# A graph layer with linear attention and expert layers on one core: where the expert jobs' results wait, and when they are scattered to the output

## The reference, cut to what matters

```
xn = layernorm(x)
x1 = x + gnn(xn, src, dst) + linear_attention(xn)
h  = layernorm(x1)
e  = argmax(h @ gate_w + gate_b)                   # one of 8 experts for each node
y  = (relu(h @ w1[e] + b1[e]) @ w2[e] + b2[e]) * prob[e]   # capacity 977 nodes an expert
out = x1 + nan_to_num(y)
```

## Time and profile before

| | |
|---|---|
| time, median of 3 runs | 1460.22 us (1460.05 to 1461.22) |
| profiled execution: its own time | 1454.21 us |
| span of its instructions | 1452.5 us |
| busy: TensorE, VectorE, ScalarE, GpSimd | 78%, 56%, 39%, 63% of the span |
| granted TensorE clock, mean | 0.914 |
| indirect DMAs: gathers, row scatters, result scatters | 784, 49, 54 |

### The profile page before, as it was taken

One profiled execution on the slowest core, in us unless ns is written; L12 is line 12 of the kernel. 1 busy time (PEld: TensorE's weight loads), 2 busy tenths in 40 slices (PEclk: granted clock), 3 DMA queues, 4 the chain that ended last, 5 costly groups with the idle time before them and its releaser, 6 DMA issues.

```text
span 1452.5 us, 34026 instructions
## 1 busy us (share of the span) xinstructions
PE 1138.5 (78%) x5961; PEld 809.4 (56%) x5962; DVE 818.0 (56%) x2766; ACT 560.9 (39%) x1458; POOL 918.9 (63%) x967
## 2 busy tenths in 40 slices
PE   2659977758778777888868888787888788888896
PEld 1437643534545445665545655565665666667885
DVE  5954432647657666666535555464665566656443
ACT  2843221322323234343423334343454444545342
POOL 3545776777777776767767676776766666751111
PEclk9569997879888989999989999899999999999998
DMA  8484333444545456545545455555555565555562
GB/s 250 139 230 154 103 106 99 146 125 146 150 143 152 146 154 190 170 140 182 163 135 162 153 178 174 166 178 164 180 171 167 183 197 165 172 161 164 162 181 83
DMA packets 143379, 231.83 MB, mean 160 GB/s; under 512 B 29824, under 2 KB 87329, under 8 KB 143248
## 3 DMA queue, kind: packets, MB, share of 16 engines
q0 software_dynamic: 42896, 115.65, 26.5%
q1 hardware_dynamic: 99118, 114.27, 25.6%
q10 hardware_dynamic: 1234, 0.66, 0.2%
HBM read 197.40 MB, written 35.08 MB: 160 GB/s over the span
## 4 chain that ended last, share of the span: by engine, by line
PE 29%; issue 26%; POOL 22%; DVE 8%; DMA 5%; ACT 4%; POOLq 3%; DVEq 2%; SPq 1%; ACTq 0%; PEldq 0%
POOL shared L587 21%; PE pY L1036 7%; PE pH L1045 6%; PE pA L915 6%; DMA shared<-table,idx 3%; DVE shared L1415 2%; PE pX L1013 1%; PE pT L967 1%; PE pQ L959 1%; DMA shared<-in_L_ffn_b_dram 1%; PE pD L973 1%; ACT w2s L651 1%; ACT w2s L646 1%; PE pH L895 1%; DVE shared L1421 1%
## 5 line engine op out<-in xcount | busy, mean ns | idle before, releaser
L587 POOL DMA_INDIRECT shared<-table,idx x784 | 766.8, 978 | 318.6 <-issue 272.4
L915 PE MATMUL pA<-shared,onehot 128*128 x976 | 281.6, 398 | 141.4 <-POOLq L567 79.9
L915 PEld LDWEIGHTS pA<-shared,onehot 128*128 x976 | 91.9, 98 | 320.0 <-issue 245.1
L1355 DVE TENSOR_TENSOR onehot<-tile_iota,dst_t 128x512 f32 x244 | 160.2, 694 | 105.8 <-PE pA L915 69.9
L1036 PE MATMUL pY<-w2s,shared 128*128 x864 | 208.3, 396 | 11.8 <-issue 9.0
L1045 PE MATMUL pH<-shared 128*128 128x128 f32 x1728 | 205.1, 278 | 6.6 <-DMA shared<-in_L_ffn_w_dram 6.6
L1045 PEld LDWEIGHTS pH<-shared 128*128 128x128 f32 x1728 | 204.0, 194 | 10.4 <-DMA shared<-in_L_ffn_w_dram 7.9
L1036 PEld LDWEIGHTS pY<-w2s,shared 128*128 128x128 f32 x864 | 165.7, 197 | 37.9 <-issue 15.7
L765 ACT ACTIVATE shared<-pH,b1s 128x128 f32<-128x128 f32 x432 | 122.2, 370 | 97.1 <-PE pH L1045 90.1
L700 ACT ACTIVATE shared<-pA 128x512 f32<-128x512 f32 x49 | 29.3, 597 | 272.2 <-PE pA L915 272.2
L1397 DVE TENSOR_SCALAR tile_iota<-tile_iota 128x128 f32<-128x128 f32 x48 | 12.7, 264 | 203.6 <-PE pA L915 203.6
(11 more groups left out here) (248 smaller groups left out, 1667.2 us busy)
## 6 DMA issues: line engine op xcount, KB each, us to landing
shared<-in_L_ffn_w_dram SPq DMA_DIRECT2D x108, 512.0 KB, 4.2
shared<-table,idx POOLq DMA_INDIRECT x784
w2s<-in_L_ffn_w_dram SPq DMA_DIRECT2D x8, 1024.0 KB, 6.8
rows<-rows_sb SPq DMA_DIRECT2D x7, 1040.0 KB, 14.6
shared<-rows SPq DMA_DIRECT2D x54, 130.0 KB
shared<-in_L_ffn_b_dram SPq DMA_DIRECT2D x54, 128.0 KB
shared<-in_x_dram SPq DMA_DIRECT2D x12, 512.0 KB, 8.7
table<-w2s SPq DMA_DIRECT2D x12, 512.0 KB, 3.1
```

The source lines that it names most:

```text
L587: g.indirect_dma_start(gathered[:, s * G + j, :], None, table[:, :], bass.IndirectOffsetOnAxis(ap=idx[:, q * G + j:q * G + j + 1], axis=0) ...
L915: m = pe.matmul(pA[:, :], onehot[:, n % OQ, j, :], gathered[:, (f % RQ) * G + j, :], start=False, stop=final and j == G - 1)
L1355: v.tensor_tensor(onehot[:, n % OQ, :, :], tile_iota[:, :].rearrange("p (a n) -> p a n", a=1).broadcast_to([P, G, P]), dst_t[:, bass.ds(ch ...
```

## The change

The results of the first 44 jobs (`KEPT = 44`: the 42 inside the steps and the tail's first two) are no longer written to the ring `fin`. VectorE writes the result of job j over `base` of tile j, which nobody reads any more by then, and its node numbers to column j of a wider `jtok`; these posts don't wait for a free buffer. GpSimd's `event` no longer ends with a `finish`. When the last row scatter has been issued, GpSimd scatters the 44 kept results one after another (`send_kept`), waiting only for each result and not for the scatter before. The ten jobs behind them use the ring of four as before; their `finish(r)` first waits until all earlier result scatters have landed.

```diff
+KEPT = J0 + LEAD - 2
...
-        jtok = sb("jtok", [P, FB], I32)
+        jtok = sb("jtok", [P, KEPT + FB], I32)
...
-            def finish(j):
-
-                g.wait_ge(S["fin_sc"], j * 16 + 16)
+            def finish(r):
+
+                g.wait_ge(S["fin_sc"], r * 16 + (KEPT + 1) * 16)
                 g.sem_inc(S["fin_free"], 1)
-                g.wait_ge(S["fin_ok"], j + 1)
+                g.wait_ge(S["fin_ok"], r + KEPT + 1)
                 hold(g, "pool_hold")
...
+            def send_kept(j):
+
+                g.wait_ge(S["fin_ok"], j + 1)
+                g.indirect_dma_start(out[:, :], bass.IndirectOffsetOnAxis(ap=jtok[:, j:j + 1], axis=0), base[:, j, :], None,
+                                     bounds_check=N - 1, oob_is_err=False).then_inc(S["fin_sc"], 16)
+
+            def event(t):
...
-                with g.If(T0 - 1 < t):
-                    finish(g.snap(done_r))
-                    g.reg_add(done_r, done_r, 1)
-                    g.sem_inc(S["pool_hold"], 1)
...
+            for j in range(KEPT):
+                send_kept(j)
             g.wait_ge(S["tail_ok"], 1)
-            end = g.value_load(last_job, min_val=J0, max_val=J0 + NX * JOBS)
-            with g.Fori(NT - T0, end + 1) as j:
-                finish(j)
+            end = g.value_load(last_job, min_val=J0 + LEAD - 1, max_val=J0 + NX * JOBS)
+            with g.Fori(0, end - (KEPT - 1)) as r:
+                finish(r)
...
-                def post(j):
+                def post(j, r=None):
...
-                    v.wait_ge(S["fin_free"], j + 1)
-                    v.sem_inc(S["dve_hold"], 1)
+                    if r is not None:
+                        v.wait_ge(S["fin_free"], j + 1)
+                        v.sem_inc(S["dve_hold"], 1)
...
-                    v.tensor_copy(jtok[:, bass.ds(j % FB, 1)], jrow[:, j % JB, C_TOK:C_TOK + 1].bitcast(I32))
-                    v.tensor_tensor(fin[:, j % FB, :], yc, jrow[:, j % JB, 0:D], ALU.add).then_inc(S["fin_ok"], 1)
+                    at_ = j if r is None else r % FB + KEPT
+                    done = base[:, j, :] if r is None else fin[:, r % FB, :]
+                    v.tensor_copy(jtok[:, bass.ds(at_, 1)], jrow[:, j % JB, C_TOK:C_TOK + 1].bitcast(I32))
+                    v.tensor_tensor(done, yc, jrow[:, j % JB, 0:D], ALU.add).then_inc(S["fin_ok"], 1)
...
-                v.sem_inc(S["fin_free"], FB - 1)
+                v.sem_inc(S["fin_free"], KEPT + FB - 1)
```

More of the change, by code:

```diff
@@ L517, in pick @@
                 g.sem_inc(S["pool_hold"], 1)
-            def finish(j):
-                g.wait_ge(S["fin_sc"], j * 16 + 16)
+            def finish(r):
+                g.wait_ge(S["fin_sc"], r * 16 + (KEPT + 1) * 16)
                 g.sem_inc(S["fin_free"], 1)
-                g.wait_ge(S["fin_ok"], j + 1)
+                g.wait_ge(S["fin_ok"], r + KEPT + 1)
                 hold(g, "pool_hold")
                 def send(b):
-                    g.indirect_dma_start(out[:, :], bass.IndirectOffsetOnAxis(ap=jtok[:, b:b + 1], axis=0),
+                    g.indirect_dma_start(out[:, :], bass.IndirectOffsetOnAxis(ap=jtok[:, KEPT + b:KEPT + b + 1], axis=0),
                                          fin[:, b, :], None,
                                          bounds_check=N - 1, oob_is_err=False).then_inc(S["fin_sc"], 16)
-                pick((g.snap(j % FB), 0), FB, send)
-            def event(t, done_r):
+                pick((g.snap(r % FB), 0), FB, send)
+            def send_kept(j):
[3 more added lines that the diff above has]
+            def event(t):
                 g.wait_ge(S["scat_done"], t * 16 + 16)
@@ L553, in load_end, with events @@
                 g.reg_add(reg, reg, -1)
-            def events(tile, tend, done_r, f):
+            def events(tile, tend, f):
                 with g.While(lambda: g.snap(tend) < f - LAG):
-                    event(g.snap(tile), done_r)
+                    event(g.snap(tile))
                     g.reg_add(tile, tile, 1)
@@ L572, in copy_idx, with gather @@
                 g.tensor_copy(idx[:, o:o + HALF], src_t[:, bass.ds((i % TURNS) * IDX + o, HALF)]).then_inc(S["idx_ok"], 1)
-            def gather(i, q, tile=None, tend=None, done_r=None):
+            def gather(i, q, tile=None, tend=None):
                 s = q % RQ
@@ L579, in gather @@
                 if q % 2 == 0 and not (first and q < RQ):
-                    events(tile, tend, done_r, f)
+                    events(tile, tend, f)
                 if q % RQ == 0:
@@ L601, in _ @@
             turns = g.value_load(rounds, min_val=TURNS, max_val=TURNS * NT)
-            with g.register("tile_no") as tile, g.register("tile_end") as tend, g.register("jobs_done") as done_r:
+            with g.register("tile_no") as tile, g.register("tile_end") as tend:
                 g.reg_mov(tile, 0)
-                g.reg_mov(done_r, 0)
                 load_end(tend, BEHIND)
                 for q in range(FIRST, BODY):
-                    gather(0, q, tile, tend, done_r)
+                    gather(0, q, tile, tend)
                 with g.Fori(1, turns) as i:
                     for q in range(BODY):
-                        gather(i, q, tile, tend, done_r)
+                        gather(i, q, tile, tend)
                 report(RQ - 1, turns * TRIPS * 16 * G)
                 with g.Fori(g.snap(tile), NT) as t:
-                    event(t, done_r)
+                    event(t)
+            for j in range(KEPT):
+                send_kept(j)
             g.wait_ge(S["tail_ok"], 1)
-            end = g.value_load(last_job, min_val=J0, max_val=J0 + NX * JOBS)
-            with g.Fori(NT - T0, end + 1) as j:
-                finish(j)
+            end = g.value_load(last_job, min_val=J0 + LEAD - 1, max_val=J0 + NX * JOBS)
+            with g.Fori(0, end - (KEPT - 1)) as r:
+                finish(r)
         @block.scalar
@@ L1650, in _ @@
                 plan(PLANNED + 1, 1.0)
-                with v.Fori(0, n) as i:
+                for i in range(LEAD - 1):
                     post(i + (J0 - 1))
                     plan(i + (PLANNED + 2), 1.0)
-                end = v.value_load(last_job, min_val=J0, max_val=J0 + NX * JOBS)
-                post(end)
+                with v.Fori(0, n - (LEAD - 1)) as r:
+                    post(r + KEPT, r)
+                    plan(r + (PLANNED + LEAD + 1), 1.0)
+                end = v.value_load(last_job, min_val=J0 + LEAD - 1, max_val=J0 + NX * JOBS)
+                post(end, v.snap(end - KEPT))
 _INS = ["x", "src", "dst", "L0_gnn_W", "L0_gnn_b", "L0_mix_wq", "L0_mix_bq", "L0_mix_wk", "L0_mix_bk", "L0_mix_wv", "L0_mix_bv",
```

## The result

The changed kernel takes 1446.7 us (median of 6 runs, 1443.8 to 1451.0), the kernel before beside it 1459.9 us (6 runs, 1451.4 to 1461.2). The ratio is 0.9917, with a 95% interval of 0.9891 to 0.9943: 13 us faster, where the prediction said 31. The time lies above the predicted range.

The account below looks back on a forecast made before the run. GpSimd, sending DMAs one after another, was taken to hold up TensorE until 1146 us, TensorE's own work after. Loop gain 34 less tail cost 3 gave 31 us off the 1460.2 us median: 1429.2 us, range 1417 to 1443.

Parts of the forecast that it names:

- the prediction's sum for the loop: Gain in GpSimd's loop from 650 to 1296 us: 19.9 to 924, 14.1 to 1146, 0 after, together 34 us.
- 19.9 were predicted up to 924 us: Loop, 650 to 924 us: 13 result scatters go, and all 19.9 us reach TensorE, which waits 34.9 us there.
- 14.1 predicted: Loop, 924 to 1146 us: TensorE gets back 7.5 us of relay waits and 6.6 us of weight waits.
- the 1.53 us each: GpSimd's busy and idle time per result scatter leaving the loop, 35 of them, 53.5 us; flag, counter and branch included.
- The tail: After the last row scatter: 44 kept scatters in a row cost 2.0 + 1.2 = 3 us, bounds 0 and 8.
- two mechanisms: In the tail: job 47 waits for the ring, TensorE 2.0 us late; scatter traffic slows four bias loads, 1.2 us.
- 2.0 predicted: In the tail: job 47's mask operation on VectorE is 6.0 us late, which makes TensorE 2.0 us late.
- 0.3 each: In the tail: scatter traffic adds 0.3 us to each of four bias loads, judged from the loop's weight loads.
- GpSimd never bound behind 1146 us: Rival on the loop: GpSimd bounds everywhere, all 35 scatters count, 53.5 - 3 = 50 us gained, 1410 us, 12%.
- The kept scatters went back to back: Rival on the tail: each kept scatter must land before the next, 2.8 us each, 24 us slower, 1484 us, 4%.
- The second rival: Loop, 924 to 1146 us: stalls recur in other steps, so 19.9 - 3 = 17 us gained, 1443 us, 13%.
- the four: All the rivals; the last: gathers are late for their landings, not GpSimd's time, 0 to 3 us slower, 1461, 3%.

Follow-up runs that it names:

- the kernel with 74 increments: The changed kernel with 74 idle semaphore increments, one instruction each, ahead of GpSimd's first gather: 1426.8 us, ratio 0.9829 to the kernel before.
- with 10 and with 60 increments: The kernel before with 10 or 60 idle semaphore increments ahead of GpSimd's first gather: 1455.5 us (ratio 0.9999) and 1471.8 us (ratio 1.0120).

## Why the prediction was wrong

**The size of the loop's gain was right for a kernel that was not the one built.** In the kernel with 74 increments TensorE's 38th step begins 35.1 us earlier than before; the prediction's sum for the loop was 34. By stage: its 24th step (892.72 us before) 20.1 us earlier, where 19.9 were predicted up to 924 us, and 14.9 more to the 38th (14.1 predicted), then nothing more: its 49th step is 34.8 us early. The events themselves freed less than the 1.53 us each, and as much in the kernel that was built: from the end of the gather ahead of an event to the start of the one behind it, 155.2 us for the last 35 events of the loop before, 118.8 after and 118.7 with 74 increments, 1.04 each; for the first 13 of them, which TensorE waits for, 54.5, 36.7 and 36.4 us, 1.39 each with 74. Cheaper turns than before (31.8 against 36.1 us) made up for part of it, so that the 35.1 us come so near to 34 is in part luck.

**The step that failed** is the sentence "The flag, the counter and one branch that leave GpSimd's loop are in the 1.53 us". It treats code that leaves a loop as time that leaves it, and the rest of the loop as unchanged. But with the branch gone from the seven event sites, the loop's head and its first gather came to lie elsewhere, and the turns up to frame 112 had a second stall. Turn by turn (excess after over before) that is 10.9 us up to frame 84, and TensorE's 12th step began 11.6 us late:
```profile
641.40 0.38 PE L938 MATMUL pA<-c 128*128 128x512 f16 x1
```
and before
```profile
629.75 0.38 PE L935 MATMUL pA<-c 128*128 128x512 f16 x1
```
From frame 98 to 140 the excess is 7.4 us, and the stage's 19.9 became 11.7 (the 24th step began as late as before, from 11.6 us behind); frames 154 and 168 add 4.4 us, and 14.1 became 10.1. Together 34 - 10.9 - 7.4 - 4.4 = 11.3 us were left, and the profile shows 10.1. Of the last 4.4 us at most 1.8 depend on the place: the two turns take 12.5 us after, 10.8 with 74 increments and 8.1 before. Why they are longer than before in that kernel too is open.

The stall ahead of the loop's head is in both kernels: after, the first instruction behind the branch back at frame 98 runs 4.1 us later, 1.56 us behind the start of a packet; before, 3.0 us later and 1.54 us behind one. The second stall made the difference.

**The tail** was mis-sized, 3 for 7 us (4 us against the 103.2 us that the kernel before takes with 10 and with 60 increments). Its two mechanisms are there. Job 47's mask operation waits for the ring, with 74 increments (for the earlier trace rows):
```profile
1370.62 0.29 DVE L1556 TENSOR_SCALAR finite<-shared 128x256 int32<-128x256 f32 x1 [6.07 <-POOLq L523]
```
and TensorE is 3.0 us later behind it (2.0 predicted; 0.5 in the profile after, where the jobs were late already). The bias loads were 0.8, 1.2 and 0.9 us slower in the profile after than before, 2.9 together, where 0.3 each had been taken from the loop's rows; before, the first two took (the third is in the earlier trace rows):
```profile
1360.11 3.93 DMA shared<-in_L_ffn_b_dram
...
1375.60 3.72 DMA shared<-in_L_ffn_b_dram
```
The loop's weight loads were a poor model for a bias load that the job hangs on. The third part was not foreseen: in 1330 to 1350 us TensorE's granted clock is 0.83 on the mean, 0.5 for 3.4 us from 1330.1 and for 3.4 us from 1343.8 and 1.0 between; TensorE had stood idle for 1.4 us until 1329.46 and for 3.3 us until 1342.82, and two output products took
```profile
1330.66 5.11 PE L1039 MATMUL pY<-w2s,shared 128*128 x16 [0.95 <-issue]
1342.82 5.40 PE L1039 MATMUL pY<-w2s,shared 128*128 x16 [3.26 <-issue]
```
instead of 3.71 us; by the time the second is over, jobs are 3.4 us later against the last row scatter than before. So of the 7 us in the profile after about half is the two mechanisms, 0.5 and 2.9, and half is this. It isn't tied to the scatters alone: the kernel before with 10 and with 60 increments has such products in its tail too (6.55 us; 5.25 and 5.40), the one without kept scatters has none. Why the clock falls in some executions is open.

**The rivals.** GpSimd never bound behind 1146 us: with 74 increments it is up to 42 us earlier (first gather of frame 195 at 1248.0, before 1289.8), and TensorE 35. Stalls for weights did not recur. The kept scatters went back to back. The second rival's 17 us are nearest to the 13 measured, by luck: what it named did not happen. None of the four named a cost of the loop's turn.

**Median and profile.** The two profiled executions are 3.2 us apart in their own times, the medians 13. Traces of the same loop in dear places put the 38th step 10.1 to 19.9 us early, so one execution is good to some 5 us here, and what is shown rests on the medians of the table and the sums of 13 turns, not on one trace's end.

## What to carry to other kernels

In this kernel GpSimd's instruction stream is on the critical path and runs a long loop, and idle instructions ahead of that loop moved the time by more than the change did: 74 of them took 20 us off the changed kernel, 60 put 1.2% on the kernel before, and the change itself gave 13 us. So compare two such kernels only after shifting each by some idle instructions, and look at the idle time at the loop's turn first. Try the work that the engine must send right behind the loop's head, and code that is mostly jumped over behind it (here the turns took 8.2 us in place of 54.9, with the head at the same instruction). And for a burst that is moved to the end, price the loads that somebody waits for there from a run with the burst (here 4.59 to 4.89 us a bias load, against 3.60 to 4.00 without), or place it where the engine and the DMA queues are idle (here that made the tail 102.6 us instead of 107.1, and a gain in the time is not shown).

## What was not expected of the hardware

Idle increments, one instruction each and 0.08 us apart, sent while GpSimd had nothing to do, made the changed kernel 16 to 20 us faster with 64, 74 and 120 of them, and changed nothing with 24 and 128 beyond what the runs can tell. The stalls they remove take, beyond the usual 0.8 to 0.9 us from slot wait to gather, 1.5 to 2.1 us each in the profile after at frames 28 to 70 and 98, where a packet of 8192 bytes on the "instruction" queue starts at most 0.7 us behind the slot wait, and 3.8 and 5.8 us at frames 84 and 112, where it starts 2.2 and 4.3 us behind. Two packets behind one branch back start 2.3 us apart at frame 98 (646.57 and 648.88). With an event's row scatter between head and gather the slot wait is 1.15 us ahead of the gather, against 0.82 us before the change.
